# First weights loaded by halves, idle products of PE in the prologue, and a new order of steps, in a four-stage transformer kernel on one core

## The reference, cut to what matters

```python
# A0: causal attention, 16 heads of 8, queries and keys through a rank of 64
q = einsum('bhtr,hrd->bhtd', einsum('btd,hdr->bhtr', x, q_a), q_b)      # k likewise
att = softmax(where(causal, q @ k.T / sqrt(8), min))
y = (att @ (x @ v_w.T + v_b)) @ o_w.T + o_b
# F0: gated FFN with ternary weights: silu(x w1) * (x w2), two hidden layers of 512 with gelu, down to 128
# A1: full attention, 16 heads of 8, W_qkv, softmax / sqrt(128), W_out
# F1: FFN of 512 with relu, a top-1 expert adds a low-rank term, down to 128
```

## Time and profile before

| | |
|---|---|
| median of three runs | 914.33 us |
| the three runs | 914.22, 914.33, 916.58 us |
| the profiled execution | 914.29 us, its span 912.6 us |
| busy share of the span | PE 95%, DVE 73%, ACT 54%, POOL 21% |
| mean granted clock of PE | 0.983 |
| DMA | 63.77 MB, mean 70 GB/s |
| instructions | 19418 |

### The profile page before, as it was taken

One profiled execution on the slowest core, in us unless ns is written; L12 is line 12 of the kernel. 1 busy time (PEld: TensorE's weight loads), 2 busy tenths in 40 slices (PEclk: granted clock), 3 DMA queues, 4 the chain that ended last, 5 costly groups with the idle time before them and its releaser, 6 DMA issues.

```text
span 912.6 us, 19418 instructions
## 1 busy us (share of the span) xinstructions
PE 871.0 (95%) x7160; PEld 688.0 (75%) x7160; DVE 670.0 (73%) x2393; ACT 493.7 (54%) x958; POOL 194.6 (21%) x395
## 2 busy tenths in 40 slices
PE   6979899999999999999999999999999999999996
PEld 4757687887768886788777887778876887778754
DVE  4666728777899579975798859994798749654864
ACT  2233456547657646643656546673565655663382
POOL 6222212002410223021500224011330224010201
PEclk9988899999999999999999999999999999999999
DMA  6432222221332024302142033210433022002200
GB/s 220 130 90 62 63 71 71 80 74 32 94 113 73 1 88 132 98 2 60 55 127 65 14 88 115 74 43 8 119 104 89 2 71 62 10 13 76 82 9 12
DMA packets 47821, 63.77 MB, mean 70 GB/s; under 512 B 5472, under 2 KB 41648, under 8 KB 43024
## 3 DMA queue, kind: packets, MB, share of 16 engines
q1 hardware_dynamic: 45472, 57.14, 21.8%
q10 hardware_dynamic: 2256, 5.40, 1.7%
HBM read 47.48 MB, written 14.29 MB: 68 GB/s over the span
## 4 chain that ended last, share of the span: by engine, by line
PE 58%; DVE 19%; issue 9%; DMA 6%; ACT 4%; SPq 2%; POOL 2%; ACTq 0%; POOLq 0%; DVEq 0%
PE banks L1152 17%; PE banks L1083 7%; PE banks L1065 7%; PE banks L1012 6%; DVE top L785 6%; PE banks L1134 4%; PE banks L1208 4%; DMA krow<-scratch 3%; DVE x L866 2%; PE banks L953 2%; PE banks L1181 2%; DVE banks L774 1%; PE banks L962 1%; PE banks L1062 1%; ACT L632 1%
## 5 line engine op out<-in xcount | busy, mean ns | idle before, releaser
L632 ACT ACTIVATE prob<-banks 128x384 f32<-128x384 f32 (+1 forms) x512 | 246.8, 554 | 108.6 <-PE banks L1065 51.4
L785 DVE TENSOR_REDUCE top<-banks 128x2 f32<-128x512 f32 (+1 forms) x268 | 166.3, 680 | 25.2 <-PE banks L1012 19.7
L1065 PE MATMUL banks<-qrow,krow 75*128 75x256 bf16 x992 | 149.3, 266 | 8.8 <-ACT prob L632 3.6
L774 DVE CUSTOM_DVE_ANT_0 banks<-banks,above 128x128 f32<-128x128 f32 x448 | 144.6, 388 | 17.6 <-PE banks L1012 14.7
L563 POOL TENSOR_TENSOR ln_rstd<-ln_var,minus_half 128x2 f32<-128x2 f32 x64 | 44.8, 703 | 421.8 <-DVE ln_var L856 421.5
L1012 PE MATMUL banks<-krow,qrow 72*128 72x256 bf16 x752 | 123.9, 275 | 2.2 <-DMA krow<-scratch 0.7
L1083 PE MATMUL banks<-prob,v 128*32 128x256 f32 (+1 forms) x2048 | 119.6, 365 | 1.9 <-POOL prob L570 1.5
L1065 PEld LDWEIGHTS banks<-qrow,krow 75*128 75x128 bf16 x992 | 88.0, 100 | 41.4 <-ACT prob L632 8.8
L1152 PE MATMUL banks<-hid,wh 128*128 128x256 f32 x512 | 117.2, 384 | 0.0
L1152 PE MATMUL banks<-glu,wh 128*128 128x256 f32 x512 | 116.6, 381 | 0.0
L1152 PEld LDWEIGHTS banks<-hid,wh 128*128 128x128 f32 x512 | 96.3, 192 | 13.4 <-issue 0.8
(11 more groups left out here) (123 smaller groups left out, 1176.6 us busy)
## 6 DMA issues: line engine op xcount, KB each, us to landing
qrow<-scratch SPq DMA_DIRECT2D x30, 576.0 KB
krow<-scratch SPq DMA_DIRECT2D x90, 192.0 KB
scratch<-split SPq DMA_DIRECT2D x93, 128.0 KB, 1.8
xt<-in_xt SPq DMA_DIRECT2D x16, 128.0 KB, 3.1
x<-in_x SPq DMA_DIRECT2D x16, 128.0 KB, 4.2
wh<-in_wh ACTq DMA_DIRECT2D x2, 1024.0 KB, 8.5
out<-xout SPq DMA_DIRECT2D x16, 128.0 KB, 1.9
qrow<-tsplit SPq DMA_DIRECT2D x90, 8.0 KB, 2.0
```

Of the source, the lines that this page charges most:

```text
L632: nc.scalar.activation(prob[s][:, j % 2, g, 0:wide], banks[:, b, 0:wide], ACT.Exp, scale=1.0 / float(np.sqrt(np.float32(HD))) if s == A0 e ...
L774: done = nc.vector.tensor_tensor_reduce(out=bank[:, g * wide:(g + 1) * wide], in0=bank[:, g * wide:(g + 1) * wide], in1=above[:, 2 * P - w ...
L785: nc.vector.tensor_reduce(out=dst, in_=src, axis=AX, op=ALU.max, negate=True).then_inc(maxed[s], 1)
L1065: done = nc.tensor.matmul(bank[:, kb * SEQ:(kb + 1) * SEQ - q0], krow[s][n % DEEP[s]][0:ROWSM, h, kb * P:(kb + 1) * P], qrow[s][n % DEEP[s ...
```

## The change

It has three parts.

1. Loads. `wqb` is loaded by halves too, each ahead of its half of `wqa`, and xt of chunk 0 (with a semaphore of its own, `first_there`) comes between the two halves. SP, no longer ACT, issues the four small loads, directly behind. x of chunk 0 is loaded as two tiles.
2. Prologue. PE does each half through to its projections before the other: fold, turn back, project. DVE follows in an order of its own, and copies `wq` last. DVE first clears a 128x128 piece of `prob` called `nothing`; PE multiplies it with itself nine times into bank 7 ahead of the first fold, and one or two times between later steps ("idle products"). ACT does one activation of one column ahead of its first wait.
3. Order. `SEQUENCE` and `BANK_TABLE` are replaced throughout. Eight letters of `KIND` are renamed (a and b change places, c and d, f and g, n and o by kind), which alone changes nothing.

```diff
@@ sync
-            sp.dma_start(wqb, d_in["qk_b"]).then_inc(weights0, DMA)
             for half, there in enumerate((weights0, weights0b)):
                 pairs = bass.ts(half, HEADS // 4)
+                sp.dma_start(wqb[:, pairs], d_in["qk_b"][:, pairs]).then_inc(there, DMA)
                 sp.dma_start(wqa[:, pairs], d_in["qk_a"][:, pairs]).then_inc(there, DMA)
+                if half == 0:
+                    sp.dma_start(xt[A0][0][:], d_in["xt"][:, 0:TOK]).then_inc(first_there, DMA)
+            sp.dma_start(wv[A0][:], d_in["v_w0"]).then_inc(weights1, DMA)
+            sp.dma_start(rows[:], d_in["rows"].partition_broadcast(P)).then_inc(weights1, DMA)
+            sp.dma_start(wo[A0][:], d_in["o_w0"]).then_inc(weights1, DMA)
+            sp.dma_start(cols[:], d_in["cols"]).then_inc(weights1, DMA)
...
+                if is_first(n):
+                    for t in range(TILES):
+                        sp.dma_start(x[A0][0][:, t], d_in["x"][bass.ts(t, P), :]).then_inc(loaded[0], DMA)
+                    return
@@ scalar
-            act.wait_ge(weights0, 2 * DMA)
-            act.wait_ge(weights0b, DMA)
-            act.dma_start(wv[A0][:], d_in["v_w0"]).then_inc(weights1, DMA)
-            act.dma_start(rows[:], d_in["rows"].partition_broadcast(P)).then_inc(weights1, DMA)
-            act.dma_start(wo[A0][:], d_in["o_w0"]).then_inc(weights1, DMA)
-            act.dma_start(cols[:], d_in["cols"]).then_inc(weights1, DMA)
+            act.wait_ge(nothing_made, 1)
+            nc.scalar.activation(tables[:], nothing[:, 0:1], ACT.Identity)
@@ vector
+            nc.vector.memset(nothing, 0.0).then_inc(nothing_made, 1)
             for i in range(2):
                 nc.vector.memset(qrow[A1][i][:].rearrange("p h t -> p (h t)").bitcast(F32), 0.0).then_inc(kf_cleared, 1)
...
+            to_wex(0)
+            to_kf(0)
+            to_wex(1)
+            to_qf(0)
+            to_kf(1)
+            to_qf(1)
+            for half in range(2):
+                nc.vector.tensor_copy(wq[A0][:].rearrange("p s (c h) -> p s h c", c=HD)[:, :, HALF * half:HALF * half + HALF],
+                                      back[half]).then_inc(wready, 1)
@@ tensor
+            def idle(times):
+
+                for _ in range(times):
+                    nc.tensor.matmul(banks[:, 7, 0:P], nothing, nothing, start=True, stop=True, skip_group_check=True)
...
+            def direct_keys(half):
+
+                pe.wait_ge(wex_ready, half + 1)
...
+            pe.wait_ge(nothing_made, 1)
+            idle(9)
+            fold(0)
+            pe.wait_ge(made, 2)
+            idle(1)
+            turn_back(0)
+            idle(1)
+            pe.wait_ge(first_there, DMA)
+            direct_keys(0)
+            fold(1)
+            idle(2)
+            turn_back(1)
+            idle(1)
+            direct_keys(1)
```

More of the change, by code:

```diff
@@ L79 @@
 KIND = {
-    "a": ("pass1", A0), "b": ("v", A0), "c": ("early", A0), "d": ("qk", A0),
-    "e": ("pass2", A0), "f": ("values", A0), "g": ("maxima", A0), "h": ("outputs", A0),
+    "a": ("v", A0), "b": ("pass1", A0), "c": ("qk", A0), "d": ("early", A0),
+    "e": ("pass2", A0), "f": ("maxima", A0), "g": ("values", A0), "h": ("outputs", A0),
     "i": ("merge", A0), "j": ("project", A0), "k": ("turn", A0), "l": ("norm", A0),
-    "m": ("osum", A0), "n": ("resid", A0), "o": ("causal", A0), "p": ("load", A0),
+    "m": ("osum", A0), "n": ("causal", A0), "o": ("resid", A0), "p": ("load", A0),
     "q": ("fetch", A0), "r": ("gated", F0), "s": ("hidden", F0), "t": ("down", F0),
@@ L278, in build @@
         one = sb("one", [P, 1])
+        tables = sb("tables", [P, 1])
         dve_carrier = sb("dve_carrier", [P, 4])
@@ L392, in build @@
         early_full = per_stage("early_full")
+        nothing_made = sem("nothing_made")
+        first_there = sem("first_there")
         early_parts = per_stage("early_parts", (A1,))
@@ L680, in _, with to_wex @@
             nc.vector.tensor_reduce(out=one[:], in_=ident[:].rearrange("p (g c) -> p g c", c=WIDE)[:, :, HD], axis=AX, op=ALU.add).then_inc(one_made, 1)
-            for half in range(2):
+            dve.wait_ge(wex_cleared, 1)
+            dve.wait_ge(kf_cleared, 2)
+            dve.wait_ge(one_made, 1)
+            back = [banks[:, 2 + half, 0:2 * D].rearrange("p (s h c) -> p s h c", s=2, c=2 * HD)[:, :, :, 0:HD] for half in range(2)]
+            def to_wex(half):
                 dve.wait_ge(folded, half + 1)
                 nc.vector.tensor_copy(turned[:, half], banks[:, half, 0:2 * D]).then_inc(kept, 1)
-            dve.wait_ge(wex_cleared, 1)
-            back = [banks[:, 2 + half, 0:2 * D].rearrange("p (s h c) -> p s h c", s=2, c=2 * HD)[:, :, :, 0:HD] for half in range(2)]
-            for half in range(2):
                 dve.wait_ge(unturned, half + 1)
@@ L689, in _, with to_kf @@
                                       back[half]).then_inc(wex_ready, 1)
-            for half in range(2):
-                nc.vector.tensor_copy(wq[A0][:].rearrange("p s (c h) -> p s h c", c=HD)[:, :, HALF * half:HALF * half + HALF],
-                                      back[half]).then_inc(wready, 1)
-            dve.wait_ge(kf_cleared, 2)
-            dve.wait_ge(one_made, 1)
-            for half in range(2):
+            def to_kf(half):
                 at, pair = slice(WIDE * (GROUP - 1), P), slice(2 * half, 2 * half + 2)
@@ L699, in _, with to_qf @@
                                         ALU.add).then_inc(qkf_made, 1)
+            def to_qf(half):
                 if half == 0:
@@ L907, in _, with fold @@
         def _(pe):
-            for half in range(2):
+            def idle(times):
+                for _ in range(times):
+                    nc.tensor.matmul(banks[:, 7, 0:P], nothing, nothing, start=True, stop=True, skip_group_check=True)
+            def fold(half):
                 if half == 0:
@@ L913, in _ @@
                 else:
-                    pe.wait_ge(weights0b, DMA)
+                    pe.wait_ge(weights0b, 2 * DMA)
                 for side in range(2):
@@ L920, in _, with turn_back @@
                 done.then_inc(folded, 1)
-            pe.wait_ge(made, 2)
-            for half in range(2):
+            def turn_back(half):
                 pe.wait_ge(kept, half + 1)
@@ L926, in _ @@
                 done.then_inc(unturned, 1)
-            pe.wait_ge(wex_ready, 2)
-            pe.wait_ge(loaded[0], 2 * DMA)
-            for half in range(2):
+            def direct_keys(half):
+                pe.wait_ge(wex_ready, half + 1)
                 for side in (1, 0):
```

105 lines of the change are left out of this document (53 added, 52 removed).

## The result

| | before | after |
|---|---|---|
| median, range (4 executions each) | 914.28 us, 913.54 to 916.58 | 903.64 us, 899.68 to 907.28 |
| profiled execution, its span | 914.29, 912.6 us | 899.68, 897.9 us |
| mean granted clock in it | 0.983 | 0.986 |

The ratio of after to before is 0.9857, 95% interval 0.9815 to 0.9899, which is 13.1 us of 914.3. The medians of these few executions differ by less, 10.6 us (0.9884); a second measurement of the same kernel (e5) gave 0.9856 [.9823, .9889], and the mean spans of all executions differ by 13.1. Executions in the slow state are left out of every ratio and mean here (two of before's, one of e3's that took 1467.5 us at a mean clock of 0.55, and one of e18's, 912.3 us, which is the one that its profile shows). The profile of after is the fastest of its four executions.

What follows compares the result with a forecast made beforehand. PE, busy 95% of 912.6 us, was taken as the bound almost everywhere, with a serial prologue. Prologue 3.8 plus order to 50 us 2.3 plus zero behind gave 6.1 less: 908.2 us, range 901.5 to 914.8 (8 in 10).

Steps and rivals of the forecast that it cites:

- R4: One early low-clock stretch vanishes as PE's idle times shrink: 901.4 to 903 us; chance 0.20 together with other good luck.
- After 50 us: Rest of the kernel behind 50 us, steady rounds included: zero gain, bounds -5 and +6.
- The prologue's 3.8: Start up to the unbroken pass 1: 3.8 us earlier, v already done; bounds 2.1 and 4.5.
- the 0.3 for fold 0: Start of the prologue: fold 0 at 5.4 us, 0.3 earlier than before; bounds 5.1 and 5.7.
- R1: Prologue: direct projections stay at the lower clock level, prologue gives 2.1, all 4.4: 909.9 us; chance 0.12.
- The order's 2.3: New step order from the prologue to 50 us: net gain 2.3 us, bounds 0.5 and 3.0.
- The two waits of 0.77 and 1.53: PE's waits from 36.5 us for DVE and before `values` at 42.19 for POOL: both disappear.
- the 0.7 kept for ACT: Before 50 us: ACT ends about 1 us behind PE, chunk 1's banks come late; 0.7 us kept for that.
- The 13.6 and 10.4 us stay: Windows 60 to 80 and 100 to 120 us: the low-clock time there, 13.6 and 10.4 us, was expected unchanged.
- The bound of -5: Steady rounds behind 50 us: most they could win, 5 us, about one avoided low-clock stretch.
- R2: Early gain is lost in a later DVE or chunk-chain stretch, or a worse-ordered round: 912 to 916 us; chance 0.19.
- R3: About 14 steady rounds each lose 0.7 us waiting for DVE or ACT between passes, 9.8 in all: 918 us; chance 0.11.

Runs made afterwards that it cites:

- e3: The change with its new step order only up to 50 us and the order of before behind: 912.49 us, ratio 0.9957.
- e18: The kernel of e15 with thirteen idle products ahead of fold 0 in place of nine: 901.33 us, ratio 0.9825.
- e1: New loads and prologue alone, with the steps and banks of before: 910.29 us, ratio 0.9941.
- e11: The change without ACT's early activation of one column: 902.0 us, executed once.
- e12: The change with qk_b loaded whole, ahead of the first half of qk_a, as before: 899.19 us, executed once.
- e6: The change without any idle product in the prologue: 911.70 us, ratio 0.9939.
- e4: The change with its new step order only up to 150 us and the order of before behind: 909.84 us, ratio 0.9936.
- e13: The kernel before, with DVE's clearing and nine idle products added ahead of its first fold: 912.33 us, ratio 0.9960.
- e2: New step order and banks alone, with the loads and prologue of before: 905.91 us, ratio 0.9906.
- e9: The change with the order of before up to 150 us and the new order behind: 909.84 us, ratio 0.9949.
- e8: The change with 21 added products in PE's waits at both early gaps: 897.79 us, ratio 0.9800.
- e16: The kernel of e8 with fourteen more products before steps of the last two chunks: 904.41 us, ratio 0.9877.
- e15: The change with 12 added products in PE's waits at both early gaps: 896.85 us, ratio 0.9797.
- e7: The change with 11 added products in the first gap alone, 52.6 to 59.3 us: 902.54 us, ratio 0.9854.
- e14: The change with ten added products in the second gap alone, ahead of chunk 2's first three pass-2 steps: 899.92 us, ratio 0.9852.
- e10: The kernel before, with the new order in one stretch alone, some 690 to 745 us: 919.2 us, executed once.

## Why the prediction was right or wrong

**It was wrong in size**: 6.1 us forecast, 13.1 by the ratio and by mean spans (913.9 to 900.8), 10.6 by the medians of the four. 903.64 lies in the range, towards R4. The step that failed is "After 50 us", the term set at zero: it measured 6.4, of which 3.5 is full-clock time and 2.9 clock loss. The terms ahead of it measured 3.5 for 3.8 and 3.3 for 2.3.

- **The prologue's 3.8: nearly right, as a sum.** e1's profile wins 3.49 (pass 1 unbroken from 15.19 against 18.68, and still 3.49 at chunk 1's), and its executions 4.3 of full-clock time. Idle products cover the wait (forecast to end at 5.1 to 5.6, measured 5.32), fold 0 at 5.60 (5.4), projections at 8.03 (7.6) and at 0.49 per product in the timeline (0.43 was a length of the chain; the timeline of before has 1.03 for two), pass 1 at 14.81 (13.8), unbroken from 16.16 (15.35). By the prediction's own count that is 18.68-16.16+0.50 = 3.0 in the new order, where pass 1 waits 0.43 for qf(1). It runs 0.4 late at the first projections, 0.6 at the second and 0.9 at qf(1), which starts at 13.97 behind the 0.76 of DVE's key copy (forecast 13.1). ACT's table load, priced as hidden, is worth nothing either way (e11), and the halves of `qk_b`, behind the 0.3 for fold 0, too (e12).
- **R1, the clock not held: refuted as the usual case, true in some.** e6 puts 4.4 us on the products. But in two of the thirteen profiles with the new prologue and its nine products, e3's and e4's, the level was lost at 8.6 and 8.7, and in e13 at 8.7. The prediction took it as one chance for all executions; it is a share of them.
- **The order's 2.3: too low.** The two waits of 0.77 and 1.53 went as forecast, and the 0.7 kept for ACT was not needed: no wait for ACT stands before chunk 1's first pass 1. That makes 3.0; measured are 3.26 (46.11 to 42.85) on the new prologue and 3.98 on the old one. With the prologue's share the sum to 43 us was 6.75 for 6.1.
- **After 50 us, zero: this failed.** "The 13.6 and 10.4 us stay" did not hold. The stretches are now 6.8 and 13.7, and one of two short ones in the tail is gone; over executions the loss is 2.9 lower. PE is not as idle there as before: the four waits of the first gap are 3.0 together where before has 4.0, the longest 1.14 in place of 2.00. And the rounds behind win: by the means, the change 10.2 less 6.75 = 3.5 of full-clock time, e2 6.4 less 3.98 = 2.4. The profiles put 1.8 to 2.4 on the order itself, between the sixth and the last parking, of which 1.8 are waits for DVE and POOL; what a single execution wins or loses beside that is waits for DMA rows. I had "no row that prefers one", yet the waits of before in these rounds could have been summed (15.2 us) as a bound on what an order can win. The bound of -5 covers the medians (3.9 behind 50 us), not the means (6.4). (The range, 901.5 to 914.8, is narrower above than the sum of all bounds: 4.5+3.0+5 gives 901.8, and 2.1+0.5-6 gives 917.7. And DVE's pieces of 0.69 overlap: in the timeline of before the twelve from 50.26 take 7.27.)
- **R2 (absorbed): refuted.** Nothing of the 6.75 is given back. **R3 (slower rounds): refuted in its sum.** Between the sixth and the last parking PE waits for ACT as long as before (2.8 to 3.0 for 2.7) and less for DVE, where R3 had 9.8 more for both.
- **R4 (a low stretch vanishes): half true.** None vanished whole of the two early ones; half of the first did, and the second is 3.4 longer.
- **The rules against the trace.** The Trainium skill (ScalarE: Activation LUTs, What ACT_TABLE_LOAD costs) adds a drain of about 1.38 us to each switch; in e11 the load is at 9.17, 1.28 long, and the next activation at 10.46. No profile here shows a drain, on a first load or on a later switch. Before's timeline, with an activation that ends at 131.39 ahead of it:

```profile
131.41 1.28 ACT L654 ACT_TABLE_LOAD   x1
132.70 0.60 ACT L654 ACTIVATE hid<-banks 128x512 f32<-128x512 f32 x1
```

- The rule of the Trainium skill on transposes (TensorE: Matmul & The Clock Gate, PE-mode transpose), that they do not count as activity for the clock, is neither shown nor refuted: in e13 the level was lost behind folds, transposes and waits, in after it was held with plain products between, and in e3 and e4 it was lost with the same plain products. Waits and transposes were not separated.

**Open.** How the 6.4 behind 50 us divide beyond the 1.8 to 2.4 of the rounds and the 2.9 of clock loss: one to two us are left, near the scatter of the means. The splices e3, e4 and e9 did not divide the gain. Why some waits of PE after a rise end in a low stretch and others don't. And the loads of the change (the xt tile early, the small loads on SP) were never tried without its prologue.

## What to carry to other kernels

Sum span x clock and span less that before comparing two versions: here about a fifth of the gain, and most of the scatter, was clock loss, and one profile of each would have hidden it. Where PE is the bound and must wait, a few products into a bank that the next step overwrites can hold its clock (twelve were worth 5 us, though not in every execution); they pay at waits that a low stretch follows, and each costs about its own length. To judge a reordered schedule, take several profiles of either order, measure a long stretch between two landmarks, and take off the clock loss and the waits that differ between executions of the same steps: here that left 2.4 us, with a gap of 1.4 between the two groups, where single profiles of the two differ by anything from -1.5 to 5.1.

## What the runs showed of the hardware that I had not expected

- Every profile has stretches at the lower level, of 3.4 to 17.1 us each, and their places and lengths differ between kernels whose steps there are the same.
- Profiles without an early low stretch have others later, at steps unchanged in the order: at 222.0 in e8 (3.4 us), 245.1 in e16, 785.2 in e15 (3.4), near 855 in e7 and e14. That one leads to the other is not shown: e1, with both early ones, has 6.8 us at 336.2, and e10 has 3.4 at 762.6.
- The clock column stands at 1.00 at the start even when PE is at its lower level (e6: 3.75 for four products at 8.64, with 1.00 in the column from 9 to 10.5). Only the spacing of products tells it, as in the earlier trace rows.
- The same load of fold 0's data landed, by PE's start, at 5.47 to 6.91 in the profiles with halves of `qk_b`, and at 5.52 to 5.68 in the five with it whole.
- PE's waits for rows that come back by DMA are 1.3 to 5.6 us in all between the sixth and the last parking, in executions of the same steps.
